# Graph network on one core: two projections moved ahead of their normalisations, and the first attention's third relation after the pair

## What is computed

```python
# block 0: twice a relational convolution (3 relations and a root), relu, and a gate against 8x64 query rows
attn = sigmoid(hg[:, :, None, :] + qg[:, None, :, :]);  qi = einsum('bnlf,blf->bnf', attn, q)
alpha = sigmoid(h3 @ Wq[:, :F].T + qi @ Wq[:, F:].T + bq);  hn = alpha * tanh(qi) + (1.0 - alpha) * h3
# block 1: graph convolution;  A is the normalised adjacency with self loops
out = A @ (x @ W) + b
# block 2: two relational attentions (4 heads, then 1) with elu between them
xr = einsum('nd,rdf->rnf', x, W);  qi = oi @ q;  kj = oj @ k          # oi, oj: rows of xr by edge
a = softmax over the edges into a node of leaky_relu(qi + kj);  out = segment_sum(a * oj) + b
# block 3: graph convolution, relu, graph convolution
```

## Time and profile before

| | us |
|---|---|
| median of 3 runs | 265.73 |
| lowest and highest | 265.25, 266.22 |
| the profiled execution's own time | 265.27 |
| its span in the profile | 263.4 |

### The profile page before, as it was taken

How to read it: one execution, slowest core, us unless ns; L and a number is a source line. 1 busy time by engine, 2 the same in 40 slices (tenths; PEclk the granted TensorE clock), 3 DMA queues, 4 the chain that set the end, 5 groups by cost and what they waited for, 6 DMA issues and landing times.

```text
span 263.4 us, 5173 instructions
## 1 busy us (share of the span) xinstructions
PE 249.2 (95%) x2161; PEld 129.2 (49%) x2161; DVE 156.2 (59%) x281; ACT 96.0 (36%) x159; POOL 84.4 (32%) x78
## 2 busy tenths in 40 slices
PE   8899999998999999899998999999999988999994
PEld 4575654444545542367765333236564443435572
DVE  0745324417887999842926688994767367405322
ACT  2323210008676996313703577871312013013000
POOL 7581000006997799400001768970000000000000
PEclk9999999999999999999999999999999999999999
DMA  6999999899701979340089900005999995000001
GB/s 233 373 402 402 400 325 185 117 366 402 304 1 24 405 290 340 25 119 2 2 298 400 377 6 2 2 0 134 387 404 403 400 341 212 0 0 2 0 2 30
DMA packets 39913, 53.48 MB, mean 203 GB/s; under 512 B 22986, under 2 KB 23754, under 8 KB 39891
## 3 DMA queue, kind: packets, MB, share of 16 engines
q1 hardware_dynamic: 29792, 51.64, 55.2%
q10 hardware_dynamic: 10098, 1.52, 3.4%
HBM read 52.17 MB, written 0.20 MB: 199 GB/s over the span
## 4 chain that ended last, share of the span: by engine, by line
PE 75%; DVE 8%; ACT 6%; DMA 4%; issue 3%; POOL 2%; SPq 1%; DVEq 0%; POOLq 0%
PE ps L1194 12%; PE ps L1310 11%; PE ps L1162 10%; PE ps L1398 7%; PE ps L1209 5%; DMA W<-in_L_gnn_Wg 4%; PE ps L1384 3%; PE ps L1374 3%; PE ps L1279 3%; PE ps L1587 3%; PE ps L1667 3%; PE ps L1138 3%; ACT pre L739 2%; POOL prod L642 2%; PE ps L1455 2%
## 5 line engine op out<-in xcount | busy, mean ns | idle before, releaser
L642 POOL TENSOR_TENSOR prod<-pre,qn 128x768 f32<-128x768 f32 x28 | 54.3, 1956 | 11.2 <-ACT pre L739 11.2
L972 DVE TENSOR_TENSOR pre<-ps,qg 128x768 f32<-128x768 f32 x46 | 43.2, 953 | 11.5 <-PE ps L1384 7.2
L739 ACT ACTIVATE pre<-pre 128x768 f32<-128x768 f32 x46 | 38.5, 848 | 6.5 <-DVE pre L972 6.4
L1310 PE MATMUL ps<-W 128*128 128x384 f32 x96 | 35.2, 492 | 0.7 <-ACT W L479 0.4
L479 ACT COPY W<-ps 128x384 f32<-128x384 f32 x35 | 16.0, 483 | 25.0 <-PE ps L1138 24.9
L1310 PEld LDWEIGHTS ps<-W 128*128 128x128 f32 x96 | 17.1, 190 | 10.3 <-issue 2.2
L1398 PE MATMUL ps<-prod,rsel 128*32 128x384 f32 x192 | 20.5, 497 | 1.3 <-DVE prod L964 0.7
L1194 PE MATMUL ps<-W,prod 128*64 128x256 f32 (+1 forms) x240 | 20.6, 328 | 0.0
L739 ACT ACTIVATE ps<-ps 128x768 f32<-128x768 f32 x18 | 14.2, 795 | 17.2 <-PE ps L1384 16.1
L1194 PEld LDWEIGHTS ps<-W,prod 128*64 128x64 f32 x240 | 15.1, 137 | 4.9 <-issue 0.5
L1138 PE MATMUL ps<-ident,W 128*128 128x128 f32 x108 | 16.6, 280 | 0.8 <-ACT W L479 0.4
(11 more groups left out here) (248 smaller groups left out, 332.6 us busy)
## 6 DMA issues: line engine op xcount, KB each, us to landing
W<-in_L_gnn_W SPq DMA_DIRECT2D x9, 2304.0 KB, 12.5
W<-in_L_gnn_W_rel SPq DMA_DIRECT2D x6, 2304.0 KB, 17.5
W<-in_L_gnn_W_root SPq DMA_DIRECT2D x2, 2304.0 KB, 16.0
W<-in_L_gnn_Wq SPq DMA_DIRECT2D x4, 1152.0 KB, 9.5
qn<-in_L_gnn_query_embs SPq DMA_DIRECT2D x4, 384.0 KB, 10.1
W<-in_L_gnn_Wg SPq DMA_DIRECT2D x3, 384.0 KB, 3.9
W<-in_L_gnn_Wg SPq DMA_DIRECT2D x1, 1152.0 KB, 9.6
W<-in_L_gnn_Wg SPq DMA_DIRECT2D x12, 96.0 KB, 3.9
```

The lines of the kernel that those rows point to most:

```text
L642: nc.gpsimd.tensor_tensor(prod_of(T), pre_of(T), qn[:, pair_and_node(t)[0], :], ALU.mult).then_inc(prod_p, 1)
L739: nc.scalar.activation(tile, tile, ACT.Sigmoid).then_inc(sig_ready, 1)
L972: nc.vector.tensor_tensor(dst, ring(T), by_half(qg[:, pair_and_node(T % TILES)[0], :]), ALU.add).then_inc(pre_ready, 1)
L1310: ins = nc.tensor.matmul(ps[:, unit_bank(u), 0:HD], qT[:, k, p * P:(p + 1) * P], WgT_q[:, k, c * HD:(c + 1) * HD], start=(k == 0), stop=(k ...
```

## The change

It has three parts, and a fourth that goes with them.

1. *Projection ahead of two normalisations.* For the inputs of blocks 1 and 3, TensorE turns and projects the tile that isn't normalised yet (`project_before_norm`, `project_raw`), while the statistics are made. The mean is taken out behind the projection: `raw = mean * (column sums of W) - y @ W` (`take_means`), and the product with the adjacency comes last, with the adjacency scaled by minus one over the root (`gcnS`, `times_adj`). The column sums of `L1_W` and `L3_W1` are made on GpSimd by five adds over the six blocks (`sum_rows`) and a matmul by ones (`sum_weights`). In block 3 ScalarE copies the tile out of PSUM first.
2. *The pair of relations first in the first attention.* Relation 2's scores no longer come from its projected nodes but from `W q` and `W k`: its matrix is loaded once more in 32x32 blocks (`L2_W1T`), turned by VectorE (`turn_w1`, two blocks before the gate's last product and four after the second normalisation) and multiplied by q and k (`w1_scores`). Its projection itself moves behind, between and after the scores.
3. *Two statistics per normalisation*, of 256 and 128 columns, in place of three of 128.
4. `V_AT` spreads the v_units over five stages, none ahead of the second normalisation and four instead of two at the start of the second attention; `L2_W2_0` is loaded later; filler matmuls go.

```diff
-            ("L1_W", 5, 1), ("L2_W1_0", 2, 1), ("L2_W1_1", 3, 1), ("L2_W1_2", 6, 1),
-            ("L2_W2_0", 4, 1), ("L2_W2_1", 0, 1), ("L2_W2_2", 1, 1), ("L3_W1", 5, 1), ("L3_W2", 2, 1)]
+            ("L1_W", 5, 1), ("L2_W1_0", 2, 1), ("L2_W1_1", 6, 1), ("L2_W1_2", 3, 1),
+            ("L2_W1T", 4, 6), ("L2_W2_0", 0, 1), ("L2_W2_1", 5, 1), ("L2_W2_2", 1, 1), ("L3_W1", 4, 1), ("L3_W2", 2, 1)]
...
-        V_AT = (3, 3, 4, len(V_UNITS) - 10)
+        V_AT = (0, 1, 4, 4, 3)
+        W1T_AT = (2, 4)
...
-            load("L2_W1_2", a["L2_gnn_W1"][2], rgcn_done, done + 4)
-            load("L2_W2_0", a["L2_gnn_W2"][0], hg_done, 2)
+            load("L2_W1_1", a["L2_gnn_W1"][1], rgcn_done, done + 4)
+            sp.wait_ge(hg_done, 2)
+            load_blocks(sp, "L2_W1T", a["L2_gnn_W1"][2], range(P // GN), range(KC))
             sp.wait_ge(reduced, TILES)
+            load("L2_W1_0", a["L2_gnn_W1"][0])
...
-            load("L2_W1_0", a["L2_gnn_W1"][0])
-            load("L2_W1_1", a["L2_gnn_W1"][1])
-            load("L2_W2_1", a["L2_gnn_W2"][1], alpha_done, 4)
+            load("L2_W1_2", a["L2_gnn_W1"][2])
+            load("L2_W2_0", a["L2_gnn_W2"][0], alpha_done, 4)
             load("L2_W2_2", a["L2_gnn_W2"][2])
-            load("L3_W1", a["L3_gnn_W1"], proj_done, 2)
-            load("L3_W2", a["L3_gnn_W2"], rel_done, 3)
+            sp.wait_ge(w_summed, 1)
+            load("L2_W2_1", a["L2_gnn_W2"][1], raw_done, 2)
+            load("L3_W1", a["L3_gnn_W1"], VT1_done, 1)
+            load("L3_W2", a["L3_gnn_W2"], rel_done, 2)
...
+            def sum_rows(key):
+
+                wait_loaded(pool, key)
+                w = W[SLOT[key]]
+                link(nc.gpsimd.tensor_tensor(w_rows, w[:, 0, :], w[:, 1, :], ALU.add))
+                for k in range(2, KC - 1):
+                    link(nc.gpsimd.tensor_tensor(w_rows, w_rows, w[:, k, :], ALU.add))
+                nc.gpsimd.tensor_tensor(w_rows, w_rows, w[:, KC - 1, :], ALU.add).then_inc(w_summed, 1)
+
+            pool.wait_ge(prod_p, pool_tiles(2 * TILES))
+            sum_rows("L1_W")
             pool.wait_ge(reduced, TILES)
             nc.gpsimd.memset(V_f, 0.0).then_inc(v_cleared, 1)
+            pool.wait_ge(w_sums_done, 1)
+            sum_rows("L3_W1")
...
+            nc.scalar.activation(small[:, 47:48], small[:, 41:42], ACT.Sqrt)
+            for part, cols in enumerate(PARTS_OF):
+                act.wait_ge(att_part, part + 1)
+                nc.scalar.copy(t1[:, cols], wide(RGAT2)[:, cols]).then_inc(y_made, 1)
             ln(3)
+            sums_out(1)
...
-                for j in (range(2), range(2, JC))[part]:
-                    link(nc.vector.bn_stats(small[:, 20 + 6 * j:26 + 6 * j], y[:, j * P:(j + 1) * P]))
+                link(nc.vector.bn_stats(small[:, 20 + 6 * part:26 + 6 * part], y[:, PARTS_OF[part]]))
...
+                    nc.vector.tensor_scalar(gcnS, gcnT[:, :], small[:, 6:7], -1.0, ALU.mult, ALU.mult).then_inc(gcn_scaled, 1)
...
+            def turn_w1(stage):
+
+                at = sum(W1T_AT[:stage])
+                for k in range(at, at + W1T_AT[stage]):
+                    dve.wait_ge(loaded["L2_W1T"][k], 16 * (P // GN))
+                    nc.vector.transpose(W1T[:, k, :], W1T[:, k, :]).then_inc(W1T_ready, 1)
...
+            def take_means(i):
+
+                dve.wait_ge(w_sums_out, i + 1)
+                for part, cols in enumerate(PARTS_OF):
+                    dve.wait_ge(raw_done, 2 * i + part + 1)
+                    nc.vector.scalar_tensor_tensor(out=raw[:, cols], in0=w_cols[i][:, cols], scalar=small[:, 2:3],
+                                                   in1=raw_psum(part), op0=ALU.mult, op1=ALU.subtract).then_inc(raw_ready, 1)
...
+            def sum_weights(i):
+
+                pe.wait_ge(w_summed, i + 1)
+                for c in range(2):
+                    ins = nc.tensor.matmul(ps[c * N:(c + 1) * N, SUM_BANK, 0:HD], small[:, 45:46].to_broadcast([P, N]),
+                                           w_rows[:, c * HD:(c + 1) * HD], start=True, stop=True, skip_group_check=True)
+                ins.then_inc(w_sums_done, 1)
+
+            def project_before_norm(y, made, n, key, turned_n):
+
+                w = W[SLOT[key]]
+                turn_group(y, ident, node_turned, (made, 1), 2, 0)
+                keep_warm(1, 4)
+                wait_loaded(pe, key)
+                pe.wait_ge(nodeT_ready, 2 * turned_n - 1)
+                project_raw(w, 0, BY_BLOCK[:2])
+                turn_group(y, ident, node_turned, (made, 1), 2, 1)
+                pe.wait_ge(ln_parts, n)
+                nc.tensor.matmul(ps[:, MEANS, 0:2], avg[:, :], small[:, 0:2], start=True, stop=True).then_inc(ln_mean, 1)
+                project_raw(w, 0, BY_BLOCK[2:4])
+                sum_weights(n // 2)
+                pe.wait_ge(nodeT_ready, 2 * turned_n)
+                project_raw(w, 0, BY_BLOCK[4:]).then_inc(raw_done, 1)
+                project_raw(w, 1).then_inc(raw_done, 1)
...
-            norm_stats(1, "L1_gnn_b")
-            turn_nodes(xa, gcnT, node_turned, made=(x_ready, 2))
+            project_before_norm(t0, x_made, 1, "L1_W", 3)
+            add_bias_wide("L1_gnn_b", GCN)
+            pe.wait_ge(x_ready, 4)
             add_nodes_wide(xa, GCN)
-            wait_loaded(pe, "L1_W")
-            project_wide(nodeT, W[SLOT["L1_W"]], GCN, (0,), first=False, waits=as_copied(nodeT_ready, 3)).then_inc(proj_done, 1)
-            project_wide(nodeT, W[SLOT["L1_W"]], GCN, (1,), first=False).then_inc(proj_done, 1)
+            for part in range(2):
+                times_adj(0, part)
...
+                project_pair(0, BY_BLOCK, as_copied(nodeT_ready, 4)).then_inc(rel_done, 1)
+                w1_scores(range(2, KC)).then_inc(VT1_done, 1)
+                project_pair(1, BY_BLOCK[:1])
+                pe.wait_ge(VT1_ready, 1)
+                for c in range(2):
+                    for j in range(JC):
+                        ins = nc.tensor.matmul(ps[:, V1_BANKS[c], j * GN:(j + 1) * GN], VT1[c * N:(c + 1) * N, j * P:(j + 1) * P],
+                                               qsel[c * N:(c + 1) * N, :], start=True, stop=True, skip_group_check=True)
+                ins.then_inc(V1_done, 1)
+                project_pair(1, BY_BLOCK[1:2])
+                pe.wait_ge(V1_ready, 1)
+                turn_pair(0)
+                project_pair(1, BY_BLOCK[2:4])
```

More of the change, by code:

```diff
@@ L140, in gnn_kernel @@
         vscratch = qn_f[:, 2 * D + KC * R * N:2 * D + KC * R * N + HD].bitcast(BF16)
+        w_rows = pre[:, 2, :]
+        w_cols = [pre[:, 3, i * HD:(i + 1) * HD] for i in range(2)]
+        raw = prod[:, 0, 0:HD]
+        gcnS = prod[:, 1, 0:P]
         score = qg_f[:, 0:HD]
@@ L1533, in _, with w1_scores @@
                 project_alpha(layer, 1, qiT, WqT_q, BY_BLOCK, True).then_inc(alpha_done, 1)
-                keep_warm(1 if layer == 0 else 10, 4)
+                keep_warm(1, 4)
+            def w1_scores(ks):
+                for k in ks:
+                    if k == 0:
+                        pe.wait_ge(qk_loaded, 64)
+                    pe.wait_ge(W1T_ready, k + 1)
+                    for c in range(2):
+                        at = c * N + k % 2 * GN
+                        ins = nc.tensor.matmul(ps[at:at + GN, VT_BANK, 0:HD], qk[:, k, 0, :], W1T[:, k, c * HD:(c + 1) * HD],
+                                               start=(k < 2), stop=(k >= KC - 2), skip_group_check=True)
+                return ins
             def norm_stats(n, name=None):
-                if n > 1:
+                if n == 2:
+                    w1_scores(range(0, 2))
+                    keep_warm(2, SPARE)
+                elif n > 1:
                     keep_warm(5, SPARE)
@@ new lines, in times_adj @@
+            def times_adj(i, part):
+                if part == 0:
+                    pe.wait_ge(gcn_scaled, i + 1)
+                pe.wait_ge(raw_ready, 2 * i + part + 1)
+                cols = PARTS_OF[part]
+                nc.tensor.matmul(wide(GCN)[:, cols], gcnS, raw[:, cols], start=False, stop=True,
+                                 skip_group_check=True).then_inc(proj_done, 1)
+            pe.wait_ge(alpha_ready, 4)
+            project_before_norm(t0, x_made, 1, "L1_W", 3)
+            add_bias_wide("L1_gnn_b", GCN)
@@ L1588, in _ @@
                                                    W[SLOT[keys[r]]][:, k, c * HD:(c + 1) * HD],
-                                                   start=(i == 0), stop=(i == KC - 1), skip_group_check=True)
-                        if c == 0 and i == 2:
-                            pe.wait_ge(X_out_v, 2 * layer + 1)
-                            pe.wait_ge(X_out_s, 2 * layer + 1)
-                            for b in range(KC):
-                                turn = nc.tensor.transpose(ps[:, 5, b * N:(b + 1) * N], X2[:, b * P:(b + 1) * P],
-                                                           ident[0:N, 0:N])
-                            turn.then_inc(X_turned, 1)
@@ L1597, in _ @@
```

(26 more changed lines are left out.)

183 lines of the change are left out of this document (122 added, 61 removed).

## The result

| | before | after |
|---|---|---|
| median, us | 265.50 (4 runs) | 271.41 (4 runs) |
| lowest and highest | 265.25, 266.22 | 271.38, 272.05 |
| the profiled execution, its span | 265.27, 263.4 | 271.38, 269.6 |

The ratio is 1.0227, 95% interval 1.0206 to 1.0247: slower, by 5.9 us. The forecast was slower by 3, at 268.7, and its wide range (261.5 to 272.3) held the time; but 271.41 lies above the 270.5 at which the forecast's own case ended.

The account below looks back on a forecast made before the run. The prediction took TensorE's queue, 75% of the chain, and what it waits for as the bound. Terms +0.1 - 1.6 + 4.9 - 0.4 gave +3.0 us on 265.27, plus 0.46 for the median: 268.7 us, range 261.5 to 272.3.

Parts of the forecast that it names:

- the forecast's own case: Whole kernel: the terms as summed, 268.7 us, with its own range 267 to 270.5; chance 0.5.
- five signs named in advance: t2-hh, hh+xa over 1 us; x after 187; X01 wait 3 or more; v_units or hx 1.5 to 2.6; L3_W1 about 219.
- First normalisation, +0.1: Last gate projection to first GCN projection: adds delay x, projection then takes 7.65 us, ending 195.2 against 195.07.
- The swap of fillers for 32-wide matmuls: Second GCN normalisation: four 32-wide matmuls replace three of five fillers, claimed to make no difference.
- First attention, -1.6: First attention's first weights to its scores: the new order takes 14.8 us instead of 16.35.
- Second sum, +4.9: Second attention's start: L3_W1 adds delay hx and v_units, so the X01 copy ends at 232.7 or 232.9, against 227.9.
- the colder TensorE: Part of a rival: after standing some 6 us, TensorE runs matmuls at 1.2 GHz, adding 1.5 to 3 us.
- Last normalisation, -0.4: Second attention's end to last projection's end: 14.2 us against 14.57, y's first part in SBUF 0.67 after 242.87.
- the rival of the larger price and colder clock: Second sum: ELU's tensor_scalar waits too, hx behind all five adds, +7.0 for 4.9: 270.8, plus colder TensorE; chance 0.15.

Follow-up runs that it names:

- e3: The changed kernel with both sums' GpSimd adds left out, a one-column memset in place of each: 264.45 us, ratio to before 0.9968.
- e1: The changed kernel with only the first sum's five adds (L1_W) left out: 271.61 us, ratio to before 1.0239.
- e2: The changed kernel with only the second sum's five adds (L3_W1) left out: 267.11 us, ratio to before 1.0055.
- e6: The changed kernel with V_AT = (1, 3, 5, 0, 3), so no v_unit between hx and the X01 copy: 271.33 us, ratio to before 1.0211.
- e4: The changed kernel with twelve more filler matmuls behind the first attention, keep_warm(16, 4) for keep_warm(4, 4): 272.12 us, ratio to before 1.0258.
- e8: The changed kernel with second sum held until hx, W1T transposes moved later, V_AT (1, 3, 5, 0, 3), root table loaded after y's copies: 266.00 us.
- e9: The kernel of e8 with eight filler matmuls instead of one behind the second gate's last projection: 265.23 us, ratio to before 1.0001.
- e11: The changed kernel with third normalisation as before, four GpSimd adds in the first sum, TensorE summing a block, hh+xa early: 263.55 us, ratio 0.9932.

## Why the prediction was right, and where its sum was off

**Right.** The sign and the mechanism: slower, because GpSimd's adds hold VectorE's instructions one add at a time. The rows that carried it (products of 946 to 1627 ns beside GpSimd) were of multiplies, and the rule read from them held for adds, scalar_tensor_tensor and the v_units alike. Of the five signs named in advance three came: t2-hh and hh+xa over 1 us, the first part of x after 187, hx and v_units of up to 2.30. The wait for X01 was 1.63 us and not 3, because TensorE was itself late and slow, and L3_W1 was down 2.3 later than said. e3 shows the cause as a whole (7 us), e1 and e2 the two places.

**Off, term by term.** The size was not right: 3.0 was forecast and 5.9 measured. Every term erred to the same side, by 0.4, 0.7, 0.7 and 0.9 us, and 0.2 more lies between the scores of the first attention and its end, where none was counted. The largest error is in the last normalisation, and not in the second sum.

- *First normalisation, +0.1:* 0.37 at the projection's end, 0.51 at the attention. The start was right within 0.3 us; the stretch from x to the end took 8.2 us, not 7.65. The first four blocks of raw projection took 2.09 where 1.74 was priced, the two products with the scaled adjacency 0.85 for 0.65. The swap of fillers for 32-wide matmuls, called no difference, was 0.14. Without the adds (e1) the attention starts 0.9 us earlier than in the kernel before, so the loss here is theirs.
- *First attention, -1.6:* -0.87. The mis-sized item is V1, priced at 0.45: its matmuls (twelve records) took 1.03; the two single blocks around it took 0.80 each for 0.67. The three third-relation blocks took 0.80 each, with no copy to wait for, as priced within 0.2.
- *Second sum, +4.9:* 5.6, and here the working failed. I let hx wait for one or two adds and the ELU's tensor_scalar for none, and moved the price of that form to a rival. It waited: 1.40 for 0.26 here, 1.48 and 1.52 in e6. The rule of the Trainium skill that the rival cited (SBUF — State Buffer, "Who interferes with whom", on the 2-port forms) says that it waits, and the trace now agrees. The other part of that rival, the colder TensorE, came too: 1.0 us on the pair, though e4 shows that v_units would have held X01 without it. That the term came near I count as partly luck, for L3_W1 landed at 221.37, not 219.1: one tensor_scalar and hx met an add each, where the rival had hx behind all five, and the other three adds met the v_units. Why it landed later, and what an earlier landing would have cost, I have not settled.
- *Last normalisation, -0.4:* +0.5. I had ScalarE's table load end 0.04 after the attention, as in the earlier trace rows, and forgot the 0.2 of the dummy root behind it, and that the load there starts when the X2 copy lets it: the copy of y began at 248.53, 0.3 after the attention. That is a third of the error. The raw projection took 0.2 more than priced, as in the first normalisation, and from the transposes of y to the end it was 5.97 us where 5.6 was priced, with the copy between them on the chain. e8 puts the load behind the copies and has 14.6 us: not a gain, a draw.

**The chances.** The time lies above the forecast's own case (to 270.5) and in the rival of the larger price and colder clock (270.8 and more), which I gave 0.15; the mechanism is the forecast's with both items of that rival in it. That the range held the time is owed to the room left for that rival, with 0.9 us to spare.

## What to carry to other kernels

Work moved to an idle GpSimd is not free if it reads SBUF: list what VectorE does beside it with two SBUF inputs, or as a tensor_scalar from SBUF to SBUF, and pay for each the rest of one GpSimd instruction. Then place it beside copies out of PSUM, or make it shorter (e8 won back 5.4 of the 5.9 us, e9 all of it, e11 1.8 more). When one of two waits is taken away, look at which other work starts at a fixed time: what e1 and e6 gained in one place was given back in the next. And a wait of TensorE can cost twice, by its length and by the slower clock behind it.
